# Regrouped PSUM banks and waits in the local blocks, row maxima ahead of the normalisation, and a merged front in a two-layer kernel

## The reference

```
mod = silu(c) @ w_mod                      -> sa, ca, ga, sb, cb, gb
ga, gb: (2*(g >= 0) - 1) * max(|g|, 0.25)
h = layernorm(x) * (1 + ca) + sa;  x = x + ga * attn(h)
h = layernorm(x) * (1 + cb) + sb;  x = x + gb * ffn(h)
```

## Time and profile before

| | us |
|---|---|
| median of 3 runs | 5260.22 |
| lowest, highest | 5258.66, 5263.18 |
| the profiled execution | 5259.56 |
| its span in the trace | 5257.8 |

### The profile page before, as it was taken

One profiled execution on the slowest core, in us unless ns is written; L12 is line 12 of the kernel. 1 busy time (PEld: TensorE's weight loads), 2 busy tenths in 40 slices (PEclk: granted clock), 3 DMA queues, 4 the chain that ended last, 5 costly groups with the idle time before them and its releaser, 6 DMA issues. The chain is left out here.

```text
span 5257.8 us, 220614 instructions
## 1 busy us (share of the span) xinstructions
PE 4656.7 (89%) x81616; PEld 3372.6 (64%) x81616; DVE 3876.4 (74%) x8260; ACT 3195.5 (61%) x6716; POOL 2753.1 (52%) x3917
## 2 busy tenths in 40 slices
PE   3558948999999999999999999999999576999996
PEld 2556736676767666676767666767676454666665
DVE  5984567777777777777777777777777566777775
ACT  1002526677777777677777677777776344777675
POOL 0004116666666666666666666666665325555552
PEclk6996979999999999999999999999999688999998
DMA  1000125554545454555454555455554003444442
GB/s 58 17 1 18 43 57 130 137 132 134 132 130 139 127 143 127 141 131 141 128 141 128 140 131 140 129 136 133 138 134 119 17 7 87 115 113 114 114 113 77
DMA packets 704914, 564.32 MB, mean 107 GB/s; under 512 B 223492, under 2 KB 629864, under 8 KB 704008
## 3 DMA queue, kind: packets, MB, share of 16 engines
q1 hardware_dynamic: 691080, 537.36, 38.5%
q10 hardware_dynamic: 13312, 22.02, 1.3%
HBM read 359.38 MB, written 200.02 MB: 106 GB/s over the span
## 5 line engine op out<-in xcount | busy, mean ns | idle before, releaser
L2134 POOL TENSOR_TENSOR L_qk<-L_cos_part,L_sin_part 128x512 f32<-128x512 f32 x896 | 1128.7, 1273 | 151.5 <-DVE L_sin_part L2012 151.0
L1797 ACT ACTIVATE L_squares<-L_ps_q 128x512 f32<-128x512 f32 x896 | 534.8, 597 | 929.2 <-PE L_ps_q L1539 922.6
L1539 PE MATMUL L_ps_q<-L_w_qkv,L_xT 128*128 128x512 f32 x1792 | 971.9, 625 | 30.0 <-DVE L_sin_part L2012 11.1
L2125 POOL TENSOR_TENSOR L_qk<-L_qk,L_rnorm 128x1024 f32<-128x1024 f32 (+1 forms) x512 | 864.0, 1688 | 17.8 <-POOL L_rnorm L2108 0.5
L1574 PEld LDWEIGHTS L_ps_t<-L_ident,L_qk 128*128 128x128 f32 x3584 | 446.1, 141 | 479.1 <-issue 374.5
L2011 DVE TENSOR_TENSOR L_cos_part<-L_ps_q,L_rot 128x512 f32<-128x512 f32 x896 | 611.0, 682 | 41.2 <-POOL L_rot L2144 31.2
L2012 DVE TENSOR_TENSOR L_sin_part<-L_ps_q,L_rot 128x512 f32<-128x512 f32 x896 | 610.9, 682 | 0.0
L2013 DVE TENSOR_REDUCE L_sumsq<-L_squares 128x8 f32<-128x512 f32 x896 | 606.7, 677 | 0.0
L2102 POOL TENSOR_TENSOR L_nw_a<-L_rnorm 128x32 f32<-128x32 f32 (+1 forms) x256 | 59.5, 232 | 993.7 <-ACT L_rnorm L1827 993.7
L1574 PE MATMUL L_ps_t<-L_ident,L_qk 128*128 128x128 f32 x3584 | 540.2, 274 | 4.4 <-POOL L_qk L2125 3.2
L1808 ACT ACTIVATE L_qkT<-L_ps_t 128x512 f32<-128x512 f32 x896 | 530.6, 592 | 15.8 <-PE L_ps_t L1574 15.7
(11 more groups left out here) (290 smaller groups left out, 8908.2 us busy)
## 6 DMA issues: line engine op xcount, KB each, us to landing
L_val<-v_rows SPq DMA_DIRECT2D x896, 260.0 KB, 3.8
v_rows<-L_val SPq DMA_DIRECT2D x384, 260.0 KB, 2.1
v_rows<-L_val SPq DMA_DIRECT2D x512, 65.0 KB, 2.0
L_rot_base<-in_rot SPq DMA_DIRECT2D x256, 128.0 KB, 2.1
v_rows<-L_val SPq DMA_DIRECT2D x128, 130.0 KB, 2.1
L_x_in<-x_rows SPq DMA_DIRECT2D x512, 32.0 KB, 1.7
mid_rows<-z SPq DMA_DIRECT2D x256, 64.0 KB, 1.6
L_f_in<-mid_rows SPq DMA_DIRECT2D x256, 64.0 KB, 2.0
```

The lines of the kernel that those rows point to most:

```text
L1539: nc.tensor.matmul(ps_q[j % 2][:, :], xT[:, parity(t), :], w_qkv[:, 0:2, 256 * j:256 * j + 256], start=True, stop=True).then_inc(S["proj_p ...
L1797: nc.scalar.activation(squares[:, j % 2, :], ps_q[j % 2][:, :], ACT.Square).then_inc(S["sq_done"], 1)
L2125: nc.gpsimd.tensor_tensor(v, v, r, ALU.mult).then_inc(S["normed"], 1)
L2134: nc.gpsimd.tensor_tensor(qk[:, t % 2, h, s, :], cos_part[:, j % 2, :], sin_part[:, j % 2, :], ALU.add).then_inc(S["added"], 1)
```

## The change

1. **Front.** The stages for zero rows and modulations are gone; `delta_attention_stage` does their work. SP loads c and w_mod, then x, then the constants, then clears the rows. PE makes the eight products ahead of everything. ACT writes the two parts that need no sign (two steps of 128x1024). DVE computes silu, then the statistics (waiting for x alone), then the gated part with four steps of 128x1024.
2. **k.** The wait for the copies of k is split in two, one for each round of squares and sums.
3. **Linear block.** The statistics, roots and `normalise_mid` of groups 0, 1 and 2 move into rounds 5, 6 and 7 of the first loop.
4. **Banks and waits of the local blocks.** The transposed probabilities go to the unused columns of the scores' banks (`P_VIEW`). Prob transposes then wait for `shifted` of the same half's softmax; masks and scores wait for `pT_done`, `att_done` and `qkT_done`; up projections, qk transposes (L0) and out transposes (L1) no longer wait for `pT_done`. In L0 the down projection goes to `ps_q[0]` (`ps_d`) and stands ahead of the feature transposes; in L1 it stands behind the prob transposes. `ready_to_project` waits ahead of the scores for what the next project needs. In L1 ACT's `prob_copy` in half C stands ahead of the gelu table load.
5. **Row maxima.** The reduction of `shift` is a function of its own, `row_maxima`, and DVE runs it ahead of `normalise` in every half.

The diff, cut to its core:

```diff
+                    for l in range(2):
+                        for b in range(2):
+                            sp.dma_start(c_in[:, 2 * l + b:2 * l + b + 1], c_rows[l][b, :].rearrange("(p o) -> p o", o=1)).then_inc(mod_in, 16)
+                        sp.dma_start(w_m[:, l, :], w_mod[l]).then_inc(mod_in, 16)
                     for b in range(2):
-                        sp.dma_start(xr[:, 16 * b:16 * b + 16, :], x_dram[b].rearrange("(t p) d -> p t d", p=128)).then_inc(loaded, 16)
+                        sp.dma_start(xr[:, 16 * b:16 * b + 16, :], x_dram[b].rearrange("(t p) d -> p t d", p=128)).then_inc(x_in, 16)
...
+                    for a in cleared:
+                        n = a.shape[0] // 2049
+                        sp.dma_start(a.rearrange("(n r) d -> n r d", r=2049)[:, 0, :], tables["zeros"][0:n, :]).then_inc(rows_cleared, 16)
+                    sp.wait_ge(rows_cleared, 32)
...
+                    act.wait_ge(product, 1)
+                    by_part = mods[:, :, :, :].rearrange("p k (j i) d -> p (k j) i d", i=3)
+                    nc.scalar.activation(by_part[:, :, 0, :], banks[:, :, 0:128], ACT.Copy).then_inc(mods_done, 1)
+                    nc.scalar.activation(by_part[:, :, 1, :], banks[:, :, 128:256], ACT.Copy, bias=1.0).then_inc(mods_done, 1)
...
+                    dve.wait_ge(x_in, 32)
                     group_stats(nc, dve, step, xr, mean, rstd, (st, mv, var, half, tmp))
+                    dve.wait_ge(mods_done, 2)
+                    raw = banks[:, :, 256:384]
+                    nc.vector.tensor_scalar(sign, raw, 0.0, 2.0, ALU.is_ge, ALU.mult).then_inc(mods_done, 1)
+                    nc.vector.tensor_scalar(mag, raw, -1.0, 0.25, ALU.mult, ALU.max).then_inc(mods_done, 1)
+                    dve.wait_ge(mods_done, 4)
+                    step(nc.vector.scalar_tensor_tensor(mag, raw, 0.25, mag, ALU.max, ALU.max))
+                    nc.vector.scalar_tensor_tensor(mods[:, :, :, :].rearrange("p k (j i) d -> p (k j) i d", i=3)[:, :, 2, :], sign, -1.0, mag, ALU.add, ALU.mult).then_inc(mods_done, 2)
+                    dve.wait_ge(mods_done, 6)
...
-                    dve.wait_ge(k_out, SUB)
                     flat = prod[:, :, :, :].rearrange("p a e x -> p (a e x)")
                     kf = ks[:, :, :].rearrange("p t d -> p (t d)")
                     for j in range(2):
+                        dve.wait_ge(k_out, SUB // 2 * (j + 1))
...
+                    if i - 5 in EARLY_MID:
+                        normalise_mid(i - 5)
...
+                    early = i - 5
+                    if early in EARLY_MID:
+                        dve.wait_ge(S["mid_done"], early + 1)
+                        statistics(4, four(xm, early))
+                    if live(i + 1) or live(i + 3) or early in EARLY_MID:
+                        roots(0, i + 3, 0 if live(i + 1) else 4, 8 if live(i + 3) or early in EARLY_MID else 4, S["roots_a"])
...
+        ps_d = ps_q[0][:, 0:256] if NS == 2 else ps_x[:, 256:512]
...
+        P_VIEW = ps_s[:, :, 256:512].rearrange("x b (i q) -> x b i q", i=2)
...
+                def ready_to_project(k, T, hf):
+
+                    t, h = item(T, hf, AT_PROJ)
+                    if live(k, t):
+                        pe.wait_ge(wq_in[h], reloads(k, t, 16))
+                        wait(pe, S["rotated"], steps_(k, t, NS * h - 2))
+
                 def project(k, T, hf, s):
 
                     t, h = item(T, hf, AT_PROJ)
                     if live(k, t):
                         j = NS * h + s
-                        pe.wait_ge(S["xT_done"], tiles_(k, t))
-                        if s == 0:
-                            pe.wait_ge(wq_in[h], reloads(k, t, 16))
-                        wait(pe, S["rotated"], steps_(k, t, j - 2))
+                        if j == 0:
+                            pe.wait_ge(S["xT_done"], tiles_(k, t))
+                        if s:
+                            wait(pe, S["rotated"], steps_(k, t, j - 2))
                         if NS == 1:
                             before, g = item(T, hf, AT_VAL + 1)
                             wait(pe, S["val_done"], halves(k, before, g))
-                        if j % 2 == 0:
+                        if j == 0:
                             wait(pe, S["mid_done"], tiles_(k, T - TO_OUT - 1))
+                        if NS == 2 and j == 2 and parity(T) == TO_FT % 2:
+                            wait(pe, S["new_done"], groups_(k, T - TO_DOWN))
                         nc.tensor.matmul(ps_q[j % 2][:, :], xT[:, parity(t), :], w_qkv[:, 0:2, 256 * j:256 * j + 256], start=True, stop=True).then_inc(S["proj_ps"], 1)
...
-                            wait(pe, S["pT_done"], halves(k, t - 1, h - 1))
+                            wait(pe, S["qkT_done"], steps_(k, t, j - 1))
...
-                            pe.wait_ge(S["pT_done"], halves(k, t, h))
+                            wait(pe, S["oT_done"], halves(k, t, h - 1))
...
-                        if NS == 2:
-                            wait(pe, S["qkT_done"], steps_(k, t + 1, NS * h + NS - 1))
-                        else:
-                            wait(pe, S["oT_done"], halves(k, t, h - 1))
-                        wait(pe, S["pT_done"], halves(k, t, h - 1))
+                        read, g = item(T, hf, AT_SOFTMAX)
+                        if live(k, read):
+                            pe.wait_ge(S["shifted"], halves(k, read, g))
                         pe.wait_ge(S["exp_done"], halves(k, t, h))
                         for i in range(4):
-                            last = nc.tensor.transpose(ps_t[2 - NS][:, 128 * i:128 * i + 128], probs[:, h, 128 * i:128 * i + 128], ident[:, :])
+                            last = nc.tensor.transpose(P_VIEW[:, i // 2, i % 2, :], probs[:, h, 128 * i:128 * i + 128], ident[:, :])
...
-                        wait(pe, S["shifted"], halves(k, t, h - 1))
+                        v, g = item(T, hf, AT_PV)
+                        if live(k, v):
+                            pe.wait_ge(S["pT_done"], halves(k, v, g))
+                            wait(pe, S["att_done"], halves(k, v, g - 1))
+                        else:
+                            wait(pe, S["shifted"], halves(k, t, h - 1))
+                        pe.wait_ge(S["qkT_done"], steps_(k, t, NS * h + NS - 1))
                         wait(pe, S["kprev_done"], count(k, t, 1, 0))
                         pe.sem_inc(S["pe_turn"], 1)
                         for a in range(NB):
                             for p in range(2):
                                 rows, v = slice(64 * p, 64 * p + 64), 0 if a == 0 and parity(t) == 0 else 1
                                 nc.tensor.matmul(S_VIEW[W * a:W * a + W, p, :, :], ident_bf[rows, 64 * p:64 * p + W], masks[rows, v:v + 1, :].to_broadcast([64, HU, 2 * W]), start=True, stop=False)
-                        pe.wait_ge(consts_in, CONSTS)
-                        pe.wait_ge(S["qkT_done"], steps_(k, t, NS * h + NS - 1))
                         kk = 1 + parity(t)
...
-                        pe.wait_ge(S["pT_done"], mine)
-                        wait(pe, S["att_done"], before)
+                        s, _ = item(T, hf, AT_SCORE)
+                        if not live(k, s):
+                            pe.wait_ge(S["pT_done"], mine)
+                            wait(pe, S["att_done"], before)
...
-                            if made == "up_ps":
-                                wait(pe, S["pT_done"], halves(k, item(T, 0, AT_PV)[0], item(T, 0, AT_PV)[1]))
+                            if made == "up_ps" and NS == 2:
+                                t, h = item(T, 0, AT_SCORE)
+                                wait(pe, S["qkT_done"], steps_(k, t, NS * h + NS - 1))
+                            elif made == "up_ps":
+                                t, h = item(T, 0, AT_OUT)
+                                wait(pe, S["oT_done"], halves(k, t, h))
...
-                        value_bank_read(k, T, 0)
+                        if NS == 2:
+                            t, h = item(T, 0, AT_PROJ)
+                            wait(pe, S["rotated"], steps_(k, t, NS * h))
+                            wait(pe, S["mid_done"], tiles_(k, T - TO_OUT - 1))
+                        else:
+                            value_bank_read(k, T, 0)
...
-                        down_projection(k, T)
                     if hf == 1 and early:
                         input_transpose(k, T)
                     prob_transposes(k, T, hf)
+                    if goes_down and early:
+                        down_projection(k, T)
                     if goes_up:
                         up_projections(k, T, (1, 2) if early else (0, 1, 2))
                     if hf == 1:
@@ -1760,8 +1777,9 @@
                         if not early:
                             input_transpose(k, T)
                     if goes_down and not early:
+                        down_projection(k, T)
                         feature_transposes(k, T)
-                        down_projection(k, T)
```

(25 more changed lines are left out.)

134 lines of the change are left out of this document (43 added, 91 removed).

## The result

| | before | changed |
|---|---|---|
| median of 4 runs, us | 5260.16 | 5305.23 |
| lowest, highest | 5258.66, 5263.18 | 5302.80, 5307.27 |
| span of the profiled run | 5257.8 | 5304.5 |
| ratio | | 1.0086, 95% interval 1.0070 to 1.0102 |

The kernel became 45 us slower. I had forecast 5247 us, and the range ended at 5300.

A forecast was written before the change was run, and what follows sets the result against it. TensorE was taken to bound the first local block (busy 3261 of 3373 us), ScalarE and VectorE its C to D chain. 5259.56 −33.0 −12.2 +8.6 (first block) +23.4 (second) = 5246.4, said as 5247; own range 5230 to 5268, full range up to 5300.

The forecast's parts named there:

- The front, k, the linear block: Stages outside the local blocks: front −28.4 us, split wait for k −4.6 (together −33.0), linear block net −12.
- the +7 of the forecast: Linear block, first loop: rounds 5 to 7 take 1.3, 1.3 and 2.4 us more, plus 2 for collisions.
- all nine moved POOL steps: Linear block: if each cost 0.95 us by the exclusion rule, 8.6 in place of 2, net −6.
- The row maximum from C to D: Local blocks, third to fourth half of a pair: row maximum lengthens the ScalarE and VectorE chain, +0.60 us per pair.
- The masks behind the copy: Local blocks, fourth half of a pair: masks and scores wait for ScalarE's probability copy, +0.11 us, bounds 0 and 0.25.
- The gains in A and B: First two halves of a pair: shorter TensorE waits, −0.49 and −0.13 us in first block, −0.13 each in second.
- rival 2: Local blocks: TensorE's gains in the first two halves go to another wait, slower, 5285 us; chance 0.23.
- Rival 1: Local blocks: the row maximum does not bite, 77 us less, 5170 us, or 5140 with another gain; chance 0.25.
- rival 3: Local blocks keep their time, since edits inside them cancel or are covered: 5215 us; chance 0.12.
- the D term: Same term as the masks behind the copy: fourth half of a pair, +0.11 us per pair, bounds 0 and 0.25.

The follow-up runs named there:

- old_local_blocks: The changed kernel with the local block stages of the kernel before, so only front, split wait for k and linear block are changed: 5225.38 us (0.9932).
- before_maxima_first: The kernel before with one thing moved, VectorE taking the row maxima ahead of the normalisation in every half: 5341.11 us (1.0167).

## Why the prediction was wrong

**The front, k, the linear block: right.** −31.3 us at the end of the sums of k (87.45 for 118.73) for −33.0, of which 28.5 were left at the first project; where the other 2.8 went is open. The linear block gave −10.7 for −12.2. Its first loop, from its first output projection to its last, became 8.1 us longer (4277.00 − 4191.98 against 4264.90 − 4187.95), for the +7 of the forecast. That holds the moved work and its collisions with POOL together, so not all nine moved POOL steps can have cost 0.95, which would have made the net −6. The `old_local_blocks` run gives these parts together 36 us, for 45 in the forecast.

**The row maximum from C to D: right in mechanism and size.** +0.60 forecast, +0.66 in the pair; all three tests (undone, alone, not in D) put its price there. Its total in the changed kernel was 72 us for 77, though not in the split that I gave: 66 for 58 in the first block, 7 for 19 in the second, where another chain stood beside it.

**The masks behind the copy: the step that failed.** The term was "+0.11, bounds 0 and 0.25", from the copy's end at 2040.40, the masks' start at 2040.36 and "a hand-over of 0.1". Measured was +0.52 in the first block and +0.60 in the second. The runs show two things in its place. One: the wait stood first of four, with four instructions of PE's queue behind it in the first block and three in the second, and the hand-over was 0.55 and 0.40, not 0.10; putting it last gives 40 to 47 us. My 0.1 came from places where the wait that blocks is the last. I had called the added waits only by name and not asked in which order they stand. Two: in the second block masks and scores had covered the copy, and weighted values had already waited for it. PE in D of that block in the kernel before:

```profile
4939.49 0.30 PE L1662 MATMUL L_ps_s<-L_masks,L_ident_bf 64*64 64x256 bf16 x4
4939.62 0.61 PE L1670 MATMUL L_ps_s<-L_qkT 64*64 64x128 f32 x16
4940.50 0.71 PE L1693 MATMUL L_ps_o<-L_val,L_probsT 128*64 128x65 f32 x16 [0.27 <-issue]
```

Serial, the work that was cover became path: 0.67 us from masks to weighted values in the changed kernel. The copy ended 0.40 us earlier after the out transposes than before (3.09 for 3.49), since those started later. So the cost is 0.40 + 0.67, less the 0.10 of the old hand-over and less 0.40, which is 0.57 of the 0.60. I had carried the first block's term over instead of working it out there.

**The gains in A and B.** −0.65 and −0.26 in the first block for −0.49 and −0.13: larger than forecast. In the second, A and B gave −0.10 and +0.03 for −0.13 each; an estimate from one block did not hold in the other.

**Rivals.** The outcome lies on the side of rival 2 (slower), above its 5285, but not by its mechanism: in the first block PE did get its gains in A and B. Rival 1 is excluded by `before_maxima_first`, rival 3 by `old_local_blocks`. The upper end of the range was set by rival 2 and not by the D term, whose bounds 0 to 0.25 left out what happened. The term's true 0.52 and 0.60, by 96 and 32 pairs, adds 55 us to the forecast of 5247 and gives 5302. That this comes so near 5305 is partly luck. In the first block the stage missed its forecast by 24 us, where the term alone makes 39: A and B had gained 0.29 a pair (28 us) more than forecast. In the second it missed by 30, where the term makes 16. A and B make 6 more there (0.19 a pair), and the rest is within what one and the same code differed by between profiles (10 us).

## What to carry to other kernels

A wait that may block belongs where the fewest instructions of the queue stand behind it, mostly last; here its place alone was worth 0.8%. Before work is made to share a PSUM bank, ask what used to run beside the copy that empties the bank: that work is now behind it. And where a step is hoisted, or anything is put ahead of another on an engine, look for the one half or phase in which that engine has no idle time; the same chain also shows what else to move out, and here moving the feature statistics, which the change had not touched, was worth 66 us.

## What the runs showed of the hardware

PE starts 0.10 to 0.15 us after a releaser when the wait for it is the last instruction of its queue, and some 0.1 us later for every queue instruction behind that wait, though none of them has anything left to wait for: 0.34 with two, 0.40 to 0.45 with three, 0.54 with four. Each shows only 51 or 32 ns, and they start 0.1 us apart. Waits of the program and instructions of the queue are not the same number: arithmetic comes on top, and several waits, or a wait and an increment, can stand in one. The idle time that the profile prints for PE (0.33) was smaller than the delay by its start times (0.51): for PE the difference of starts between two like halves is the better measure.
